# Two layer normalizations written by ScalarE with a scale and a bias from VectorE, in a gated cross-attention and mixture-of-experts kernel

## The chip, the cores and the metric

The kernel runs on one core of a Trainium2 chip. The metric is the device time of one execution in microseconds, as a median over runs. A second number, the span, is the time from the first to the last instruction in the trace of one profiled execution.

## What is computed

64 sequences of 128 tokens, 128 channels wide, go through a gated cross-attention and then a gated mixture of experts, each ahead of it a layer normalization. Cut to what matters:

```
def _layernorm(x, axis=-1, eps=1e-05):
    m = jnp.mean(x, axis=axis, keepdims=True)
    v = jnp.var(x, axis=axis, keepdims=True)
    return (x - m) / jnp.sqrt(v + eps)
...
x = x + jnp.tanh(g_xattn[0]) * _L0_xattn_ref(_layernorm(x, axis=-1), ctx_768, ...)   # 16 heads, 77 keys
x = x + jnp.tanh(g_ffn[0]) * _L0_ffn_ref(_layernorm(x, axis=-1), ...)
# _L0_ffn_ref: scores = softmax(flat @ router_w.T + router_bias); top 4 of 32 experts per token,
# their outputs weighted and summed, plus a shared expert
```

## The kernel before, in words

The program has two stages. In the first one (to about 571 us) a software pipeline goes over the 64 sequences, called batches here; the change touches this stage alone. The second stage reads the tokens back sorted by expert.

Each engine runs its own function `step(i, u, has)` for i from -2 to 66: the first six and the last seven steps are written out, the 56 between them are a hardware loop with four steps in its body. In one step the engines work on batches of different age: the normalization of batch i+2, keys and values of batch i+1, the scores of batch i, softmax and context of batch i-1, the second normalization of batch i-2, the routing of batch i-3. An engine takes its instructions in the order in which `step` writes them, and each waits for semaphores (`need(engine, semaphore, count)`). So the order in a step is fixed by hand, and an instruction that waits holds up all behind it on its engine.

The names that matter:

- First normalization: DVE gets mean and variance (`mv1`), ACT makes `rs1 = exp(-0.5 ln(var + eps))`, POOL subtracts (`xc`) and multiplies (`xn`). PE transposes `xn` one step later (L987).
- Second normalization: DVE makes `mv2`, ACT `rs2`, DVE writes four copies of the normalized rows into `payload[:, u]` (L753), one of two buffers. That write waits for `sent[u]`: the four scatters of the batch two before it, which read this buffer, must have landed.
- Routing of batch i-3: PE transposes `payload` (L976), ACT copies the result to `x2T`, PE multiplies with the router weights, DVE takes the top four, makes `onehot`, PE counts positions (L1012), DVE makes `pos`, POOL `prod`, DVE `slotf` and `slot`. POOL then scatters the four copies into `x_rows` by indirect DMA (L432).
- The order on PE in one step: scores (L968), transposition of `payload` (L976), keys and values (L958), the first of three groups of probability transpositions (L920), router (L982), transposition of `xn` (L987), the rest, and last the context matmuls (L943, L948).
- L987 writes the PSUM bank `ps_f` that also held keys and values, so it waits until DVE has copied these into `kvbd` (L679).
- On ACT the copy of the values into `vt` and `vtail` (L539, L543) waits for the last context matmul of the step (L948), as that reads the old ones.

Of the kernel before, what the change touches and what calls it, by code (L numbers as in the profile page):

```python
# [29 lines left out]
E, H = 32, 128  # L30
# [40 lines left out]
def build(nc, x, ctxT, wkv, wts, vecs, consts, gu, dn, out):  # L71
# [4 lines left out]
    with ExitStack() as stack:  # L76
        def sb(name, shape, dt=F32):
            return stack.enter_context(nc.sbuf_tensor(name, shape, dt))
# [4 lines left out]
        def sems(name, n=2):  # L83
# [28 lines left out]
        xc = sb("xc", [128, D])  # L112
# [23 lines left out]
        idxf = sb("idxf", [128, TOPK])  # L136
# [59 lines left out]
        names = ("st1_d mv1_d lv1_d rs1_d xc_d xn_d xnT_p xnT_d kv_p kv_d q_p q_d vt_p vt_d s_p mx_d mxc_d diff_d relu_d "  # L196
                 "pt_p pt_d pv_p rden_d on_d oT_p oT_d y_p xb_d x1_d st2_d mv2_d lv2_d rs2_d x2_d x2T_p x2T_d x2Ta_d "
                 "lg_p lg_d top_d ntop_d idx_d idxf_d oh_d pre_p pos_d base_d prod_d slotf_d slot_d e4_d "
                 "rse_d gate_d pidx_d dest_d")
        S = {n: sem(n) for n in names.split()}  # L200
        (st1_d, mv1_d, lv1_d, rs1_d, xc_d, xn_d, xnT_p, xnT_d, kv_p, kv_d, q_p, q_d, vt_p, vt_d, s_p, mx_d, mxc_d, diff_d,
         relu_d, pt_p, pt_d, pv_p, rden_d, on_d, oT_p, oT_d, y_p, xb_d, x1_d, st2_d, mv2_d, lv2_d, rs2_d,
         x2_d, x2T_p, x2T_d, x2Ta_d, lg_p, lg_d, top_d, ntop_d, idx_d, idxf_d, oh_d, pre_p, pos_d, base_d, prod_d,
# [181 lines left out]
        def _(pool):  # L385
# [9 lines left out]
            def step(i, u, has):  # L395
# [4 lines left out]
                if has(0):  # L400

                    need_first(pool, xn_d, i + 1)
                    xi = x_all[:, bass.ds(i * D, D)]
                    nc.gpsimd.tensor_tensor(xi, xi, bias2[:, :], ALU.add).then_inc(xb_d, 1)
                if has(2):
                    m = i + 2
                    need(pool, rs1_d, m + 1)
                    need(pool, xnT_p, m - 1)
                    need_first(pool, xn_d, m)
                    nc.gpsimd.tensor_tensor(xc[:, :], x_all[:, bass.ds(m * D, D)],  # L410
                                            mv1[:, u, 0:1].broadcast_to([128, D]), ALU.subtract).then_inc(xc_d, 1)
                    need(pool, xc_d, m + 1)
                    nc.gpsimd.tensor_tensor(xn[:, u, :], xc[:, :], rs1[:, u:u + 1].broadcast_to([128, D]),
                                            ALU.mult).then_inc(xn_d, 1)
                if has(-3):
                    m, v = i - 3, o

                    need(pool, pos_d, m + 1)
                    nc.gpsimd.tensor_tensor(prod[:, :, :], onehot[:, :, :],
                                            pos[:, :].unsqueeze(1).broadcast_to([128, TOPK, E]),  # L420
                                            ALU.mult).then_inc(prod_d, 1)
# [7 lines left out]
                                            ALU.add).then_inc(dest_d, 1)  # L429
                    need_first(pool, slot_d, m + 1)  # L430
# [29 lines left out]
        def _(act):  # L460
# [8 lines left out]
            def step(i, u, has):  # L469
# [64 lines left out]
                if has(0):  # L534
                    relu(1)
                if has(1):
# [9 lines left out]
                    r.then_inc(vt_d, 1)  # L546
                if has(-2):
# [64 lines left out]
        def _(dve):  # L612
# [25 lines left out]
            def step(i, u, has):  # L638
# [571 lines left out]
```

## Time and profile before

| | |
|---|---|
| device time, median of 3 runs | 1083.81 us (1083.36 to 1087.75) |
| the profiled execution: its own time | 1080.21 us |
| its span | 1078.3 us |
| mean granted TensorE clock | 0.976 |
| busy share of the span: PE, DVE, POOL, ACT | 88%, 68%, 63%, 57% |

The shares are averages over two stages with different limits; what the change is worth is read from the first stage alone. L12 is line 12 of the kernel's file, PE is TensorE's matmuls, PEld its weight loads, DVE VectorE, ACT ScalarE, POOL GpSimd. "x_rows<-payload,slot" reads: writes `x_rows`, reads `payload` and `slot`.

### The profile page before, as it was taken

The page shows a single profiled execution, that of the slowest core. Times are in us where ns is not written, and L with a number is a line of the kernel's source. Part 1 is how long each engine was busy: PE and PEld are TensorE (multiplying, and loading weights), DVE is VectorE, ACT ScalarE, POOL GpSimd, SP SyncE. Part 2 cuts the span into 40 slices and gives each one's busy share as a digit, 9 for nine tenths or more (in the row PEclk, how much of TensorE's full clock was granted, in tenths as well). Part 3 has the DMA queues.
Part 4 walks back from the last instruction along what each step waited for, and adds up shares of the span by engine and source line. Part 5 has one row for each costly group of instructions (what it writes and reads, how often), then busy time and mean ns, then how long its engine had stood idle before and what let it go on. Part 6 is the DMA issues. An engine that isn't in the chain of part 4 may idle for free.

```text
span 1078.3 us, 26023 instructions
## 1 busy us (share of the span) xinstructions
PE 954.1 (88%) x6592; PEld 727.2 (67%) x6593; DVE 736.7 (68%) x2513; ACT 613.7 (57%) x2213; POOL 682.5 (63%) x947
## 2 busy tenths in 40 slices
PE   4998888888888988888868999999999999999976
PEld 2777777777777777777654766666676676766544
DVE  3788898898888988988755444444444444444796
ACT  3676677777667777777531555555555555554111
POOL 1276777777767777777666476777777777777000
PEclk9999999999999999999869899999999999999999
DMA  5511111111111111112213333333333333330893
GB/s 157 194 40 33 34 39 38 33 39 38 33 33 37 40 33 36 38 35 73 100 37 99 97 99 93 93 93 90 95 93 94 92 93 93 91 96 23 299 363 118
DMA packets 90278, 90.42 MB, mean 84 GB/s; under 512 B 21277, under 2 KB 71562, under 8 KB 89860
## 3 DMA queue, kind: packets, MB, share of 16 engines
q1 hardware_dynamic: 72452, 55.34, 18.0%
q0 software_dynamic: 17792, 34.67, 9.9%
q8 instruction: 17, 0.28, 0.1%
q14 instruction: 17, 0.14, 0.0%
HBM read 49.72 MB, written 42.31 MB: 85 GB/s over the span
## 4 chain that ended last, share of the span: by engine, by line
PE 43%; issue 16%; DVE 16%; DMA 12%; POOL 10%; ACT 1%; POOLq 1%; SPq 0%; DVEq 0%; ACTq 0%
PE ps L1072 11%; DMA x_rows<-payload,slot 11%; POOL x_rows L432 9%; PE ps L1083 9%; DVE payload L753 3%; PE ps L1109 3%; PE ps L1067 3%; PE ps L1077 3%; PE ps L1099 3%; PE ps L1093 3%; PE ps L1036 2%; DVE kvbd L679 2%; PE ps L1045 2%; PE ps L943 1%; DVE x_all L886 1%
## 5 line engine op out<-in xcount | busy, mean ns | idle before, releaser
L450 POOL DMA_INDIRECT y_rows<-y_sb,xin x288 | 283.1, 983 | 127.6 <-issue 81.9
L432 POOL DMA_INDIRECT x_rows<-payload,slot x256 | 251.2, 981 | 130.2 <-DVE slot L764 67.9
L839 DVE TENSOR_TENSOR h<-sg,ps 128x128 f32<-128x128 f32 x288 | 82.8, 288 | 183.7 <-ACT sg L577 183.7
L1072 PE MATMUL ps<-w_gu,xT 128*128 x576 | 175.7, 387 | 8.3 <-issue 8.3
L1083 PEld LDWEIGHTS ps<-w_dn,hT 128*128 128x128 f32 x576 | 94.3, 189 | 106.0 <-ACT hT L582 73.5
L943 PE MATMUL ps<-vt,pT 128*128 128x108 f32 x1024 | 146.1, 288 | 0.0
L943 PEld LDWEIGHTS ps<-vt,pT 128*128 128x128 f32 x1024 | 131.0, 200 | 11.6 <-issue 11.2
L582 ACT COPY hT<-ps 128x128 f32<-128x128 f32 x288 | 76.4, 265 | 109.6 <-PE ps L1077 107.9
L1083 PE MATMUL ps<-w_dn,hT 128*128 x576 | 129.9, 307 | 8.0 <-DVE y_sb L845 6.0
L577 ACT ACTIVATE sg<-ps 128x128 f32<-128x128 f32 x288 | 80.5, 279 | 72.7 <-PE ps L1072 48.6
L845 DVE TENSOR_SCALAR y_sb<-ps,xin 128x128 f32<-128x128 f32 x288 | 100.0, 347 | 24.1 <-PE ps L1083 22.5
L476 ACT ACTIVATE prob<-prob 128x512 f32<-128x512 f32 x128 | 80.5, 630 | 61.7 <-DVE prob L713 60.2
L488 ACT ACTIVATE pT<-ps 128x512 f32<-128x512 f32 (+1 forms) x192 | 99.7, 519 | 7.7 <-PE ps L920 5.1
L668 DVE TENSOR_REDUCE mx<-ps 128x8 f32<-128x616 f32 x128 | 101.1, 789 | 4.2 <-PE ps L968 3.9
L713 DVE SCALAR_TENSOR_TENSOR prob<-ps,mxc 128x616 f32<-128x616 f32 x128 | 99.6, 779 | 0.1
L1072 PEld LDWEIGHTS ps<-w_gu,xT 128*128 128x128 f32 x576 | 87.8, 193 | 11.6 <-issue 11.6
L920 PE MATMUL ps<-cst,prob 128*128 128x128 f32 x512 | 81.4, 283 | 0.3 <-ACT pT L488 0.3
L1067 PE MATMUL ps<-cst,xin 128*128 128x128 f32 x288 | 79.2, 275 | 2.7 <-DMA xin<-x_rows 2.2
L572 ACT COPY xT<-ps 128x128 f32<-128x128 f32 x288 | 78.3, 272 | 5.4 <-PE ps L1067 5.4
L1077 PE MATMUL ps<-cst,h 128*128 128x128 f32 x288 | 78.8, 274 | 0.0
L987 PE MATMUL ps<-cst,xn 128*128 128x128 f32 x64 | 21.6, 337 | 59.3 <-DVE kvbd L679 59.3
L562 ACT ACTIVATE ssg<-ps 128x512 f32<-128x512 f32 x32 | 19.1, 597 | 81.2 <-PE ps L1036 81.2
(136 smaller groups left out, 2011.9 us busy)
## 6 DMA issues: line engine op xcount, KB each, us to landing
xin<-x_rows SPq DMA_DIRECT2D x288, 65.0 KB, 1.8
w_gu<-y_rows SPq DMA_DIRECT2D x16, 1024.0 KB, 7.7
y_rows<-y_sb,xin POOLq DMA_INDIRECT x288, 2.3
w_gu<-in_gu SPq DMA_DIRECT2D x2, 2048.0 KB, 9.6
x_rows<-payload,slot POOLq DMA_INDIRECT x256, 2.4
out<-x_all SPq DMA_DIRECT2D x16, 256.0 KB, 5.0
w_dn<-in_dn SPq DMA_DIRECT2D x1, 2048.0 KB, 8.5
ctx_sb<-in_ctxT SPq DMA_DIRECT2D x64, 29.2 KB
```

The lines of the kernel that those rows point to most:

```text
L432: nc.gpsimd.indirect_dma_start(x_rows, bass.IndirectOffsetOnAxis(ap=slot[:, v, k:k + 1], axis=0), payload[:, v, k, :], None).then_inc(sent ...
L450: nc.gpsimd.indirect_dma_start(y_rows, bass.IndirectOffsetOnAxis(ap=xin[:, u, D:D + 1].bitcast(U32), axis=0), y_sb[:, u, :], None, bounds_ ...
L488: nc.scalar.activation(pT[:, f, 0:n, :].rearrange("p a b -> p (a b)"), ps_p[:, 0:n * T], ACT.Exp, scale=-1.0).then_inc(pt_d, 1)
L668: nc.vector.reduce_max(mx[:, 2 * GH * n:2 * GH * (n + 1)].rearrange("p (g a) -> p g a", a=GH), ps[:, 2 * n:2 * n + 2, 0:GK].rearrange("p g ...
L713: nc.vector.scalar_tensor_tensor(out=prob[:, u, 2 * n:2 * n + 2, :].rearrange("p g (a k) -> p g a k", a=GH), in0=ps[:, 2 * n:2 * n + 2, 0: ...
L839: nc.vector.tensor_tensor(h[:, u % 2, :], sg[:, u % 2, :], ps_gu[u % 2][:, H:2 * H], ALU.mult).then_inc(h_d[u % PER], 1)
L845: nc.vector.tensor_scalar(y_sb[:, u % U3, :], ps_dn[:, 0:D], xin[:, u % U3, D + 1:ROW], None, ALU.mult).then_inc(y_d[u % PER], 1)
L943: r = nc.tensor.matmul(ps_o[:, at:at + 3 * GC], pT[:, f, n, :], vt[:, o, c, near:near + 3, :].rearrange("p g c -> p (g c)"), start=f == 0 ...
L1067: after(nc.tensor.transpose(ps_xT[:, 0:128], xin[:, u % U3, 0:D], ident), xin_in, n16, u).then_inc(xT_p[u % PER], 1)
L1072: after(nc.tensor.matmul(ps_gu[u % 2][:, 0:2 * H], xT[:, u % 2, :], w_gu[:, bass.ds(e * (2 * H), 2 * H)], start=True, stop=True), xT_d, n, ...
L1077: after(nc.tensor.transpose(ps_hT[:, 0:128], h[:, u % 2, :], ident), h_d, n, u).then_inc(hT_p[u % PER], 1)
L1083: after(nc.tensor.matmul(ps_dn[:, 0:D], hT[:, u % 2, :], w_dn[:, bass.ds(e * D, D)], start=True, stop=True), hT_d, n, u).then_inc(dn_p[u % ...
```

## The change

Both normalizations are applied by ACT in one instruction each, `Identity(scale * x + bias)`, with the per-row `rs` as scale and a per-row bias `nb = -mean * rs` that DVE makes in one small instruction. POOL loses `xc` and `xn`; DVE loses the write of `payload`, and with it the wait for `sent[u]`, which now stands ahead of ACT's write. On POOL the step of `dest` (the index field of the scattered row) stands ahead of `prod`. DVE compares with the unsigned top indices directly, without a cast to `idxf`. ACT's `relu_tails` of batch i runs at the end of step i instead of at the start of step i+1. PE's program is the same.

```
@@ gpsimd step @@
                 if has(0):
-                    need_first(pool, xn_d, i + 1)
+                    need(pool, xn_d, i + 1)
                     xi = x_all[:, bass.ds(i * D, D)]
                     nc.gpsimd.tensor_tensor(xi, xi, bias2[:, :], ALU.add).then_inc(xb_d, 1)
-                if has(2):
-                    m = i + 2
-                    need(pool, rs1_d, m + 1)
-                    need(pool, xnT_p, m - 1)
-                    need_first(pool, xn_d, m)
-                    nc.gpsimd.tensor_tensor(xc[:, :], x_all[:, bass.ds(m * D, D)],
-                                            mv1[:, u, 0:1].broadcast_to([128, D]), ALU.subtract).then_inc(xc_d, 1)
-                    need(pool, xc_d, m + 1)
-                    nc.gpsimd.tensor_tensor(xn[:, u, :], xc[:, :], rs1[:, u:u + 1].broadcast_to([128, D]),
-                                            ALU.mult).then_inc(xn_d, 1)
...
-                    need(pool, pos_d, m + 1)
-                    nc.gpsimd.tensor_tensor(prod[:, :, :], onehot[:, :, :], ...
...
                     nc.gpsimd.tensor_tensor(dest[:, v, :], dest[:, 1 - v, :], cst[:, C_STEP:C_STEP + TOPK],
                                             ALU.add).then_inc(dest_d, 1)
+                    need(pool, pos_d, m + 1)
+                    nc.gpsimd.tensor_tensor(prod[:, :, :], onehot[:, :, :], ...
@@ scalar step @@
+                if has(2):
+                    m = i + 2
+                    need(act, nb1_d, m + 1)
+                    need(act, xnT_p, m - 1)
+                    nc.scalar.activation(xn[:, u, :], x_all[:, bass.ds(m * D, D)], ACT.Identity, bias=nb1[:, u:u + 1],
+                                         scale=rs1[:, u:u + 1]).then_inc(xn_d, 1)
                 if has(1):
                     need(act, vt_p, i + 2)
                     need(act, pv_p, FILLS * i)
...
                     r.then_inc(vt_d, 1)
+                if has(-2):
+                    m = i - 2
+                    need(act, nb2_d, m + 1)
+                    need(act, sent[u], upto(m, u, 64))
+                    nc.scalar.activation(payload[:, u, :, 0:D],
+                                         x_all[:, bass.ds(m * D, D)].unsqueeze(1).broadcast_to([128, TOPK, D]),
+                                         ACT.Identity, bias=nb2[:, :], scale=rs2[:, :]).then_inc(x2_d, 1)
+                if has(0):
+                    relu_tails()
@@ vector step @@
-                if has(-3):
-                    need(dve, idx_d, i - 2)
-                    nc.vector.tensor_copy(idxf[:, :], idx[:, 0:TOPK]).then_inc(idxf_d, 1)
...
+                if has(2):
+                    m = i + 2
+                    need(dve, rs1_d, m + 1)
+                    need(dve, xn_d, m - 1)
+                    nc.vector.tensor_scalar(nb1[:, u:u + 1], mv1[:, u, 0:1], -1.0, rs1[:, u:u + 1], ALU.mult,
+                                            ALU.mult).then_inc(nb1_d, 1)
...
                     need(dve, rs2_d, m + 1)
-                    need(dve, sent[u], upto(m, u, 64))
-                    nc.vector.tensor_scalar(payload[:, u, :, 0:D], xi.unsqueeze(1).broadcast_to([128, TOPK, D]),
-                                            mv2[:, 0:1], rs2[:, :], ALU.subtract, ALU.mult).then_inc(x2_d, 1)
+                    need(dve, x2_d, m)
+                    nc.vector.tensor_scalar(nb2[:, :], mv2[:, 0:1], -1.0, rs2[:, :], ALU.mult,
+                                            ALU.mult).then_inc(nb2_d, 1)
```

On ACT, in the hardware loop, the end of a step before (`prob` is the second half of the softmax's relu, `vt` and `vtail` the copies of the values; REGISTER_ALU and ISA rows prepare counts and addresses; numbers at the end of names are left out, so `nb` is `nb1` or `nb2`):

```order
L476 ACTIVATE prob<-prob 128x2x256
L220 REGISTER_ALU
L539 COPY vt<-ps 128x8x32
L543 COPY vtail<-ps 52x2x32 x2
L551 COPY x2T<-ps 128x128
L552 ISA
L552 COPY x2T_all<-ps 128x128
```

And of the change, the same place:

```order
L466 ACTIVATE prob<-prob 128x2x256
L528 ISA
L528 ACTIVATE xn<-x_all,nb,rs 128x128
L220 REGISTER_ALU
L533 COPY vt<-ps 128x8x32
L537 COPY vtail<-ps 52x2x32 x2
L545 ISA
L545 ACTIVATE payload<-x_all,nb,rs 128x4x128
L471 ACTIVATE ptail<-prob 128x4x52
L554 COPY x2T<-ps 128x128
```

`xn` has come in ahead of the copies of the values, `payload` and the tails (`ptail`, before at the start of the next step) between these copies and `x2T`, which copies what PE makes of `payload`.

On DVE, in the hardware loop, the end of a step before:

```order
L713 SCALAR_TENSOR_TENSOR prob<-ps,mxc 128x616
L748 RECIPROCAL rse<-se 128x1
L220 REGISTER_ALU
L753 TENSOR_SCALAR payload<-x_all,mv,rs 128x4x128
L758 TENSOR_REDUCE slotf<-prod 128x4
L761 TENSOR_SCALAR payload<-e,rse,tg 128x4
L764 CAST slot<-slotf 128x4
```

And of the change:

```order
L713 SCALAR_TENSOR_TENSOR prob<-ps,mxc 128x616
L754 RECIPROCAL rse<-se 128x1
L759 TENSOR_SCALAR nb<-mv,rs 128x1
L764 TENSOR_REDUCE slotf<-prod 128x4
L767 TENSOR_SCALAR payload<-e,rse,tg 128x4
L770 CAST slot<-slotf 128x4
```

The write of 512 numbers a row has become one of a single number, and `slot` no longer stands behind a wait for scatters.

On POOL, in the hardware loop, a step before:

```order
L404 TENSOR_TENSOR x_all<-x_all,bias 128x128
L220 REGISTER_ALU
L410 ISA
L410 TENSOR_TENSOR xc<-x_all,mv 128x128
L413 TENSOR_TENSOR xn<-xc,rs 128x128
L419 TENSOR_TENSOR prod<-onehot,pos 128x128
L425 CAST payload<-dest 128x4
L428 TENSOR_TENSOR dest<-dest,cst 128x4
L432 DMA x_rows<-payload,slot 266368x130 x4
```

And of the change:

```order
L404 TENSOR_TENSOR x_all<-x_all,bias 128x128
L410 CAST payload<-dest 128x4
L413 TENSOR_TENSOR dest<-dest,cst 128x4
L416 TENSOR_TENSOR prod<-onehot,pos 128x128
L422 DMA x_rows<-payload,slot 266368x130 x4
```

Two instructions are gone, and `prod` is now the last one ahead of the scatters.

## Rows read from the trace of the kernel before

**Rows 1.** Busy us of PE, PEld, DVE, ACT, POOL; granted clock; DMA share; GB/s.

```profile
200.00:280.00 80.00, 71.11 (x640) 59.24 (x640) 70.83 (x269) 57.26 (x197) 59.83 (x100) 1.00 0.12 37
```

**Rows 2.** POOL in order of time: start us, us, line, [idle before <-releaser].

```profile
206.65 1.04 POOL L432 DMA_INDIRECT x_rows<-payload,slot  x1 [0.95 <-DVE slot L764]
...
211.50 0.47 POOL L404 TENSOR_TENSOR x_all<-x_all,bias 128x128 f32 x1
...
212.76 0.43 POOL L419 TENSOR_TENSOR prod<-onehot,pos 128x128 f32<-128x128 bf16 x1
213.13 0.39 POOL L425 CAST payload<-dest 128x4 uint32<-128x4 f32 x1
213.60 0.20 POOL L428 TENSOR_TENSOR dest<-dest,cst 128x4 f32<-128x4 f32 x1
214.75 1.04 POOL L432 DMA_INDIRECT x_rows<-payload,slot  x1 [0.95 <-DVE slot L764]
```

**Rows 3.** The chain that ended last, one link: start us, us.

```profile
210.53 2.29 DMA x_rows<-payload,slot
```

**Rows 4.** DVE in order of time, the same step and the next.

```profile
212.91 0.56 DVE L753 TENSOR_SCALAR payload<-x_all,mv,rs 128x512 f32 x1 [0.76 <-DMA x_rows<-payload,slot]
...
213.78 0.16 DVE L764 CAST slot<-slotf 128x4 uint32<-128x4 f32 x1
...
215.74 0.79 DVE L679 TENSOR_TENSOR kvbd<-ps,cst 128x616 f32<-128x616 f32 x1
...
218.04 0.27 DVE L699 CAST idxf<-idx 128x4 f32<-128x4 uint32 x1
...
220.05 0.77 DVE L713 SCALAR_TENSOR_TENSOR prob<-ps,mxc 128x616 f32<-128x616 f32 x1
```

**Rows 5.** PE in order of time, one step from its end to its end.

```profile
212.41 0.58 PE L948 MATMUL ps<-vtail,pT 128*128 128x72 f32 x4
...
213.65 0.33 PE L976 MATMUL ps<-cst,payload 128*128 128x128 f32 x1
213.87 0.64 PE L958 MATMUL ps<-ctx_sb,wkv_sb 97*128 97x77 f32 x4
...
216.58 0.33 PE L987 MATMUL ps<-cst,xn 128*128 128x128 f32 x1 [1.49 <-DVE kvbd L679]
...
221.02 0.58 PE L948 MATMUL ps<-vtail,pT 128*128 128x72 f32 x4
```

**Rows 6.** Groups by line, 100 to 440 us: busy us, mean ns | idle before.

```profile
L476 ACT ACTIVATE prob<-prob 128x512 f32<-128x512 f32 x82 | 51.7, 630 | 41.2 <-DVE prob L713 40.1
...
L753 DVE TENSOR_SCALAR payload<-x_all,mv,rs 128x512 f32 x41 | 24.0, 587 | 23.6 <-DMA x_rows<-payload,slot 23.1
...
L521 ACT ACTIVATE qT<-ps,bq_s 128x128 f32<-128x128 f32 x42 | 15.2, 361 | 0.0
...
L497 ACT ACTIVATE lv<-mv,eps 128x1 f32<-128x1 f32 x42 | 12.3, 294 | 2.3 <-DVE mv L663 2.3
...
L499 ACT ACTIVATE rs<-lv 128x1 f32<-128x1 f32 x42 | 8.5, 203 | 1.3
...
L693 DVE TENSOR_SCALAR ntop<-top 128x1 f32<-128x1 f32 x42 | 6.5, 154 | 1.4
```

**Rows 7.** ACT in order of time, the copies of the values and a relu.

```profile
213.03 0.37 ACT L539 COPY vt<-ps 128x256 f32<-128x256 f32 x1 [0.29 <-PE ps L948]
213.30 0.42 ACT L543 COPY vtail<-ps 52x64 f32<-52x64 f32 x2
...
220.85 0.63 ACT L476 ACTIVATE prob<-prob 128x512 f32<-128x512 f32 x1
```

**Rows 8.** ACT's copies of the values in step 2 and in step 59.

```profile
42.23 0.37 ACT L539 COPY vt<-ps 128x256 f32<-128x256 f32 x1 [0.49 <-PE ps L948]
...
508.09 0.37 ACT L539 COPY vt<-ps 128x256 f32<-128x256 f32 x1 [0.29 <-PE ps L948]
```

**Rows 9.** One of four stretches alike, columns as ahead.

```profile
84.60:88.00 3.40, 3.40 (x17) 3.27 (x17) 2.77 (x11) 1.67 (x6) 2.77 (x5) 0.50 0.18 58
```

More of the change, by code:

```diff
@@ L111, in build @@
         rs1 = sb("rs1", [128, 2])
-        xc = sb("xc", [128, D])
+        nb1 = sb("nb1", [128, 2])
+        nb2 = sb("nb2", [128, 1])
         xn = sb("xn", [128, 2, D])
@@ L135, in build @@
         idx = sb("idx", [128, 8], U32)
-        idxf = sb("idxf", [128, TOPK])
         onehot = sb("onehot", [128, TOPK, E], BF16)
@@ L195, in build @@
         ctx_in, sent = sems("ctx_in"), sems("sent")
-        names = ("st1_d mv1_d lv1_d rs1_d xc_d xn_d xnT_p xnT_d kv_p kv_d q_p q_d vt_p vt_d s_p mx_d mxc_d diff_d relu_d "
-                 "pt_p pt_d pv_p rden_d on_d oT_p oT_d y_p xb_d x1_d st2_d mv2_d lv2_d rs2_d x2_d x2T_p x2T_d x2Ta_d "
-                 "lg_p lg_d top_d ntop_d idx_d idxf_d oh_d pre_p pos_d base_d prod_d slotf_d slot_d e4_d "
+        names = ("st1_d mv1_d lv1_d rs1_d nb1_d xn_d xnT_p xnT_d kv_p kv_d q_p q_d vt_p vt_d s_p mx_d mxc_d diff_d relu_d "
+                 "pt_p pt_d pv_p rden_d on_d oT_p oT_d y_p xb_d x1_d st2_d mv2_d lv2_d rs2_d nb2_d x2_d x2T_p x2T_d x2Ta_d "
+                 "lg_p lg_d top_d ntop_d idx_d oh_d pre_p pos_d base_d prod_d slotf_d slot_d e4_d "
                  "rse_d gate_d pidx_d dest_d")
         S = {n: sem(n) for n in names.split()}
-        (st1_d, mv1_d, lv1_d, rs1_d, xc_d, xn_d, xnT_p, xnT_d, kv_p, kv_d, q_p, q_d, vt_p, vt_d, s_p, mx_d, mxc_d, diff_d,
-         relu_d, pt_p, pt_d, pv_p, rden_d, on_d, oT_p, oT_d, y_p, xb_d, x1_d, st2_d, mv2_d, lv2_d, rs2_d,
-         x2_d, x2T_p, x2T_d, x2Ta_d, lg_p, lg_d, top_d, ntop_d, idx_d, idxf_d, oh_d, pre_p, pos_d, base_d, prod_d,
+        (st1_d, mv1_d, lv1_d, rs1_d, nb1_d, xn_d, xnT_p, xnT_d, kv_p, kv_d, q_p, q_d, vt_p, vt_d, s_p, mx_d, mxc_d, diff_d,
+         relu_d, pt_p, pt_d, pv_p, rden_d, on_d, oT_p, oT_d, y_p, xb_d, x1_d, st2_d, mv2_d, lv2_d, rs2_d, nb2_d,
+         x2_d, x2T_p, x2T_d, x2Ta_d, lg_p, lg_d, top_d, ntop_d, idx_d, oh_d, pre_p, pos_d, base_d, prod_d,
          slotf_d, slot_d, e4_d, rse_d, gate_d, pidx_d, dest_d) = S.values()
@@ L429, in step @@
                                             ALU.add).then_inc(dest_d, 1)
+                    need(pool, pos_d, m + 1)
+                    nc.gpsimd.tensor_tensor(prod[:, :, :], onehot[:, :, :],
+                                            pos[:, :].unsqueeze(1).broadcast_to([128, TOPK, E]),
+                                            ALU.mult).then_inc(prod_d, 1)
                     need_first(pool, slot_d, m + 1)
@@ L478, in relu_tails @@
                 def relu_tails():
-                    need(act, diff_d, 2 * i)
+                    need(act, diff_d, 2 * i + 2)
                     need(act, pt_p, FILLS * (i - 1))
-                    nc.scalar.activation(ptail[:, o, :, 0:TAIL], prob[:, o, :, 128 * CH:GK], ACT.Relu,
+                    nc.scalar.activation(ptail[:, u, :, 0:TAIL], prob[:, u, :, 128 * CH:GK], ACT.Relu,
                                          scale=-1.0).then_inc(relu_d, 1)
@@ L705, in step @@
                     m = i - 3
-                    need(dve, idxf_d, m + 1)
+                    need(dve, idx_d, m + 1)
                     need(dve, pre_p, m)
                     nc.vector.tensor_tensor(onehot[:, :, :], iota.unsqueeze(1).broadcast_to([128, TOPK, E]),
-                                            idxf[:, :].unsqueeze(2).broadcast_to([128, TOPK, E]),
+                                            idx[:, 0:TOPK].unsqueeze(2).broadcast_to([128, TOPK, E]),
                                             ALU.is_equal).then_inc(oh_d, 1)
```

9 lines of the change are left out of this document (2 added, 7 removed).

## The prediction

> **What bounds the kernel now.** I read the stretches first: in the middle of the first stage PE is busy 71.1 us of 80, DVE 70.8, ACT 57.3, POOL 59.8 [rows 1]. No engine is full, two are near it, so the period of a step must come from a ring of waits. The chain that ended last names the ring, and the timeline gives its links. First scatter of a batch at 206.65 on POOL, of the next at 214.75 [rows 2]: a step takes 8.10 us. In between, the fourth scatter's transfer starts at 210.53 and takes 2.29 [rows 3], to 212.82; DVE, idle for 0.76 us, then writes `payload` from 212.91 to 213.47, and after `slotf` and the gate `slot` ends at 213.94 [rows 4]; 0.81 us later POOL starts the next first scatter. 3.88 + 2.29 + 0.09 + 0.56 + 0.47 + 0.81 = 8.10, closed. PE has slack in it: it waits 1.49 us ahead of L987 for `kvbd` [rows 5].
>
> **What the change takes out.** DVE's `payload` write, 0.59 us [rows 6], and its wait leave DVE; `slot` no longer stands behind the scatters' landing, so this ring opens. The cast to `idxf` (0.27 us in rows 4, on a step's DVE path) goes, `nb1` and `nb2` come, 0.15 us each like `ntop` [rows 6]; for DVE alone a gain of about 0.6 us a step with the wait not counted. POOL loses `xc` and `xn`, the whole stretch between the add's end at 211.97 and `prod` at 212.76 [rows 2]: 0.8 us. Work alone gives no new bound: ACT's 57.3 of 80 us is 5.8 us in a step of 8.10, and `xn` and `payload` (below) bring it to 7.1.
>
> **What it adds, and where that lands.** The two writes go to ACT. Relu over 512 numbers takes ACT 0.63 us there [rows 6, 7]. The new write also carries a bias and a scale from memory. A bias costs 0.09: Ln with one takes 294 ns, Exp without 203 on the same one-number rows [rows 6]. A scale from memory has no row; it lies between nothing and, as the nearest row, another 0.09, and I take that, being the same kind of operand. So `payload` 0.63 + 0.18 = 0.81 us (0.72 without a price for the scale, 0.63 with none for either), and `xn` as `qT`, which has a bias, 0.36 + 0.09 = 0.45 [rows 6].
>
> The Trainium skill ("ScalarE: Activation LUTs", What ACT_TABLE_LOAD costs) gives 93 ns for each operand read per partition, and 186 ns plus 0.833 ns an element for the rest. The bias rows agree, no row shows the scale; by that page `payload` would be an estimated 0.80 us and the sum below 0.01 less. Its Rules for kernel authors there say that add and multiply belong on VectorE, not ScalarE; the write at 0.59 on DVE against 0.81 points the same way, and the first rival shows when that would not matter.
>
> Price is not the point, place is. On ACT `payload` stands behind the copies of the values, and those wait for PE's last context matmul, L948: it ends at 212.99, `vt` starts at 213.03 [rows 5, 7]. PE's next instruction but the scores is L976, which reads `payload`; queued behind it are L958 (keys and values), the probability turns, the router and L987. DVE's `kvbd` waits for L958, L987 for `kvbd`. Before, DVE wrote `payload` apart from all that, and PE reached L976 at 213.65 after its scores with the tile ready. Now there is a ring through three engines, from L948 to the next L948:
>
> - L948 to `vt` 0.04; both `vtail` end at 213.72, 0.69 after `vt` starts [rows 5, 7];
> - `payload` on ACT 0.81;
> - to L976: between 0.05 (`kvbd` ends 216.53, L987 starts 216.58) and 0.18 (`payload` ended 213.47, L976 started 213.65, with PE's scores before it) [rows 4, 5]. The second is this very wait, so I take 0.15;
> - L976 to the end of L958, 213.65 to 214.51: 0.86;
> - to `kvbd` 0.05 as above, `kvbd` 0.79, to L987 0.05;
> - L987 to the end of L948, 216.58 to 221.60: 5.02, in which PE's own order sets the pace [rows 5].
>
> Sum 8.46 us. Every link is an engine's order or a semaphore the code has, so a step can't be shorter. It leaves `kvbd`, which before had DVE's order as its limit (L958 was over at 214.51, `kvbd` began at 215.74), waiting for PE, and hides what DVE gained: DVE now idles ahead of `kvbd`. The wait for the scatters isn't the last on ACT: they land at 212.82, 0.90 ahead of the end of `vtail` at 213.72, and earlier from now on. POOL's gain only lengthens its wait for `slot`.
>
> **The stage.** From step 2 to step 59 the copies of the values move from 42.23 to 508.09 us [rows 8]: 465.86 us for 57 steps, a mean of 8.17. That holds the start at under 8.10 (no scatter to wait for yet) and the slower steps where the granted clock was 0.50, the lower level of 1.2 GHz: four stretches of 3.4 us [rows 9], 13.6 us in which PE does half as much, 6.8 us late at most; as the new ring has PE in it, I count all of it. After: 57 x 8.46 + 6.8 = 489.0, 23.1 more. In the last seven steps and the second stage nothing else changes; behind the last attention `payload` is on the path with `nb2` ahead of it, 0.15 + 0.81 - 0.59, about 0.4 us in each of two steps, 1 us. Sum +24 us. The profiled execution's own 1080.2 us would become 1104.2; the median of the runs is 3.6 above it, so 1083.8 + 24 = 1108. The small prices are each at the upper one of their two ends, so I round to 1107.
>
> **Rivals.**
>
> 1. *The open ring pays, faster.* If `payload` were written by the time PE ends its scores, PE would lose nothing, and the next ring is POOL's: four scatters to the add, 206.65 to 211.50, 4.85; add 0.47; index and `dest` 0.47 + 0.20; `prod`, now last, 0.43; 0.05 to DVE; `slotf` to `slot` 0.47; 0.81 to the scatter [rows 2, 4]: 7.75, that is 0.35 less a step, 57 x 0.35 = 20, so about 1064 us. For it: POOL and DVE are relieved, and were in the ring. It decides where `payload` ends under 0.66 us after L948 (212.99 to 213.65); the copies of the values ahead of it alone take 0.73. Chance 0.05.
> 2. *Operands cost nothing.* `payload` 0.63, 0.05 to L976: a step of 8.18, 57 x 8.18 + 6.8 = 473.1, +7 and the 1: 1092. With one operand priced, 8.27 to 8.37, 1097 to 1103. Against: the Ln row. Chance 0.17 for 1090 to 1103.
> 3. *ACT is late by itself.* From `kvbd` (215.74) DVE runs to the end of the second `prob`, 220.82 [rows 4]: 5.08, less the cast's 0.27, plus `nb1`'s 0.15: 4.96. Relu 0.03 later, 0.63, then `xn` 0.45, then `vt`; two ends overlap by 0.1 as `vt` and `vtail` do [rows 7]. With the way back to `kvbd` (0.69 + 0.81 + 0.15 + 0.86 + 0.05): 8.43, and 8.63 without the overlap. At 8.63 the stage takes 498.7, +33 and the 1: 1118. Chance 0.08 above 1116.
> 4. *No change within 0.5%.* The wait for the scatters goes over to ACT and holds the same 8.10. That needs a landing 0.9 us later than now or a period that PE's slack of 1.49 swallows; the ring above has already spent that slack. Chance 0.06.
>
> The forecast itself, steps of 8.37 to 8.6, has 0.64.
>
> **How the numbers follow.** The range takes rival 2's bound at the low end, 1091, and rival 3's at the high end, 1116; outside lie rivals 1 and 4, the tail of 3 and a little of 2, about 2 in 10. What a measurement here can tell from no change is about 0.5%, 5.4 us. Slower by more: the forecast, rival 3 and nearly all of rival 2, 0.88. Within: rival 4 and the lowest end of 2, 0.07. Faster: 0.05.
>
> **What would show it.** In the changed trace: scatters of successive batches about 8.4 to 8.5 us apart; ACT's `payload` at 0.8 us, right behind `vtail`, with no wait for a DMA; PE idle ahead of L976 (PE there waits for ACT's `payload`, about 1.0 us: it comes 0.04 + 0.69 + 0.81 + 0.15 after L948, where the scores end 0.66 after it) and less than before ahead of L987; DVE idle ahead of `kvbd`, on PE, where it had no idle time; no wait of DVE for scatters; POOL waiting longer for `slot`. I am wrong if scatters come every 7.8 us, if PE never waits at L976, or if the chain still goes through the landing of `x_rows`.

## The result, and the profile after

The changed kernel takes 1134.4 us (1132.17 to 1135.3) against 1084.28 us, both medians of four runs: a ratio of 1.0451, with a 95% interval of 1.0428 to 1.0474. That is slower, as forecast, but by 50 us where 23 were forecast, and outside the range of 1091 to 1116.

The profiled execution took 1132.17 us, with a span of 1130.0 and a mean granted clock of 0.960 (before 0.976). Its page: busy time, the granted clock in 40 slices, and three groups (busy, mean ns | idle before, releaser):

```profile
PE 981.1 (87%) x6592; PEld 745.3 (66%) x6593; DVE 739.3 (65%) x2513; ACT 687.1 (61%) x2341; POOL 625.6 (55%) x819
...
PEclk9999899899998998999987999999999999999999
...
L422 POOL DMA_INDIRECT x_rows<-payload,slot x256 | 251.5, 982 | 179.9 <-DVE slot L770 116.2
...
L682 DVE TENSOR_TENSOR kvbd<-ps,cst 128x616 f32<-128x616 f32 x64 | 51.2, 799 | 67.7 <-PE ps L964 67.7
...
L982 PE MATMUL ps<-cst,payload 128*128 128x128 f32 x64 | 21.1, 330 | 70.6 <-ACT payload L545 70.6
```

The waits have changed places as forecast: PE waits for ACT's `payload` (70.6 us over 64 steps, 1.1 each), DVE's `kvbd` waits for PE (67.7), and between steps 2 and 59 nobody waits for scatters to land (ACT's `payload` does in two later steps, 2.69 and 0.83 us). What is new is the row of the clock: in the first stage four slices read 8, where before none did; the low ones at its end, 8 and 7, were there before as 8, 6 and 8.

The copies of the values in step 2 and in step 59 bound the first stage [rows 8]:

```profile
41.82 0.37 ACT L533 COPY vt<-ps 128x256 f32<-128x256 f32 x1
...
559.38 0.35 ACT L533 COPY vt<-ps 128x256 f32<-128x256 f32 x1
```

517.56 us for 57 steps against 465.86, 51.7 more. The span grew by 51.7 too (1130.0 against 1078.3). So the whole loss lies in these 57 steps, a mean of 9.08 us, and the task is to split it.

One step at full clock, link by link. PE in order of time, from the end of L954 (the last context matmul, L948 before) to the next (start us, us, line):

```profile
249.22 0.58 PE L954 MATMUL ps<-vtail,pT 128*128 128x72 f32 x4
...
251.66 0.33 PE L982 MATMUL ps<-cst,payload 128*128 128x128 f32 x1 [1.13 <-ACT payload L545]
251.82 0.57 PE L964 MATMUL ps<-ctx_sb,wkv_sb 97*128 97x77 f32 x4
...
253.29 0.33 PE L993 MATMUL ps<-cst,xn 128*128 128x128 f32 x1 [0.31 <-DVE kvbd L682]
...
257.89 0.58 PE L954 MATMUL ps<-vtail,pT 128*128 128x72 f32 x4
```

ACT in the same step:

```profile
250.09 0.35 ACT L533 COPY vt<-ps 128x256 f32<-128x256 f32 x1
250.34 0.42 ACT L537 COPY vtail<-ps 52x64 f32<-52x64 f32 x2
250.79 0.81 ACT L545 ACTIVATE payload<-x_all,nb,rs 128x512 f32 x1
...
257.85 0.63 ACT L466 ACTIVATE prob<-prob 128x512 f32<-128x512 f32 x1
258.38 0.48 ACT L528 ACTIVATE xn<-x_all,nb,rs 128x128 f32 x1
258.77 0.35 ACT L533 COPY vt<-ps 128x256 f32<-128x256 f32 x1
```

And DVE:

```profile
252.44 0.80 DVE L682 TENSOR_TENSOR kvbd<-ps,cst 128x616 f32<-128x616 f32 x1 [1.08 <-PE ps L964]
...
254.89 0.61 DVE L708 TENSOR_TENSOR onehot<-cst,idx 128x128 bf16<-128x128 f32 x1
...
257.05 0.77 DVE L713 SCALAR_TENSOR_TENSOR prob<-ps,mxc 128x616 f32<-128x616 f32 x1
```

The forecast ring is there: `payload` follows `vtail` on ACT, takes the 0.81 us that were forecast, PE's L982 starts 0.06 after it, L964 ends 0.73 later, `kvbd` starts 0.05 later. The first link is the one that reads otherwise. L954 ends at 249.80 and `vt` could start at 249.84; it starts at 250.09, 0.29 after that end, and no wait for PE stands beside it. ACT was busy with `xn`. The same a step later (258.47 and 258.77): `xn` stands behind the second relu, and this behind DVE's second `prob`, which ends at 257.82. So ahead of `vt` the path of the third rival ends last, from `kvbd` over DVE and ACT. On it one instruction is twice its length: `onehot` takes 0.61 us where it took 0.29.

The groups of DVE and of ACT between 100 and 530 us show the means (columns as in [rows 6]):

```profile
L703 DVE TENSOR_SCALAR mxc<-mx 128x16 f32<-128x16 f32 x48 | 20.3, 422 | 1.7
L708 DVE TENSOR_TENSOR onehot<-cst,idx 128x128 bf16<-128x128 f32 x48 | 17.5, 364 | 0.0
...
L730 DVE TENSOR_SCALAR nb<-mv,rs 128x1 f32<-128x1 f32 x48 | 9.6, 200 | 0.0
```
```profile
L545 ACT ACTIVATE payload<-x_all,nb,rs 128x512 f32 x47 | 38.3, 814 | 1.2
L528 ACT ACTIVATE xn<-x_all,nb,rs 128x128 f32 x47 | 22.5, 478 | 0.0
```

And the same two DVE groups of the kernel before, 100 to 460 us:

```profile
L708 DVE TENSOR_TENSOR onehot<-cst,idxf 128x128 bf16<-128x128 f32 x44 | 12.7, 289 | 0.0
...
L703 DVE TENSOR_SCALAR mxc<-mx 128x16 f32<-128x16 f32 x44 | 7.7, 175 | 0.0
```

`mxc` is the same instruction in both kernels and takes 0.42 us in place of 0.18; `onehot` 0.36 in place of 0.29. Together 0.32 us a step, on the path that ends last ahead of `vt`. POOL in another step and in the one above shows beside what:

```profile
217.47 0.96 POOL L422 DMA_INDIRECT x_rows<-payload,slot  x1 [0.30 <-issue]
218.45 0.46 POOL L404 TENSOR_TENSOR x_all<-x_all,bias 128x128 f32 x1
...
254.54 0.96 POOL L422 DMA_INDIRECT x_rows<-payload,slot  x1 [0.30 <-issue]
255.53 0.46 POOL L404 TENSOR_TENSOR x_all<-x_all,bias 128x128 f32 x1
```

`onehot` (254.89 for 0.61) ends at 255.50, and so does the fourth scatter of the batch on POOL (254.54 for 0.96); POOL's add starts 0.03 later. In the other step it is `mxc`:

```profile
217.94 0.49 DVE L703 TENSOR_SCALAR mxc<-mx 128x16 f32<-128x16 f32 x1
218.23 0.33 DVE L708 TENSOR_TENSOR onehot<-cst,idx 128x128 bf16<-128x128 f32 x1
```

It ends at 218.43, as the scatter does (217.47 for 0.96). Between 50 and 560 us `mxc` or `onehot` is lengthened by over 0.05 us and ends like this in 49 of 56 steps. In the kernel before, in this stage, one of 56 `mxc` and none of the `onehot` was; but 12 of the 56 casts to `idxf` were, up to 0.27 us from 0.16, and the one in [rows 4] is one of these.

PE is delayed by it too: its matmuls that count positions (L1018, L1012 before) load `onehot`. One row of the waits of PEld between 100 and 520 us (us in total, times, longest), where the kernel before has none for this line:

```profile
PEld ps L1018 <- issue: 5.6, 24, 0.3
```

"issue" doesn't name the releaser, but the times do. In the steps at full clock L1018 starts 0.40 to 0.41 us after `onehot` ends, whenever that end lies over 2.0 us behind the start of `xn`'s transposition on PE (L993), and the last context matmul ends 2.57 us after that start of L1018: with `onehot` ending 2.04 us behind L993 the stretch from L993 to the end of the step is 5.01, with 2.24 it is 5.21. With an earlier `onehot` the stretch stays at 5.02.

The second part is the clock. One of 18 stretches alike between steps 2 and 59 (columns as in [rows 1]; before there were four [rows 9]):

```profile
206.89:210.30 3.41, 3.41 (x18) 3.29 (x18) 3.05 (x11) 1.65 (x6) 2.34 (x5) 0.50 0.17 52
```

In the 26 steps that have no such stretch in them or in the step ahead, the period is a mean of 8.75 us. Its links, as means over these steps, beside the forecast's and those of three experiments below (worked out from the starts and ends of the same lines):

| link | forecast | after | `prod` first | `xn` behind | ring alone |
|---|---|---|---|---|---|
| last context matmul to `vt` | 0.04 | 0.27 | 0.17 | 0.04 | 0.04 |
| `vt` to `payload` | 0.69 | 0.70 | 0.70 | 0.72 | 0.72 |
| `payload` | 0.81 | 0.81 | 0.81 | 0.81 | 0.82 |
| to its transposition on PE | 0.15 | 0.07 | 0.07 | 0.07 | 0.09 |
| to the end of keys and values | 0.86 | 0.82 | 0.82 | 0.82 | 0.81 |
| to the end of `kvbd`, and to `xn`'s transposition | 0.89 | 0.89 | 0.89 | 0.89 | 0.89 |
| to the end of the last context matmul | 5.02 | 5.17 | 5.02 | 5.13 | 5.04 |
| sum | 8.46 | 8.73 | 8.48 | 8.48 | 8.41 |
| period measured | | 8.75 | 8.48 | 8.48 | 8.40 |

In the kernel after, five of the seven links stand within 0.01 us of the forecast or under it; the first and the last are longer. 57 x 8.75 = 498.8; the other 18.8 us of the 517.56 are the steps at the lower level of 1.2 GHz, about 1.0 us for each of the 18 stretches.

So three things stood to be told apart: the ring through ACT's `payload`, the lengthened DVE instructions beside POOL's scatter, and the clock.

### The profile page after: what moved, and what is told of

Its sections match the earlier page's. It is cut to its first block, busy times and chain, and to the rows that moved or that the text cites. A ratio compares the mean times of both kernels' runs of the same rounds, so it can differ in the third digit from the quotient of the medians.

```text
span 1130.0 us, 26020 instructions
## 1 busy us (share of the span) xinstructions
PE 981.1 (87%) x6592; PEld 745.3 (66%) x6593; DVE 739.3 (65%) x2513; ACT 687.1 (61%) x2341; POOL 625.6 (55%) x819
## 4 chain that ended last, share of the span: by engine, by line
PE 52%; DVE 20%; issue 13%; ACT 9%; POOL 3%; DMA 2%; ACTq 1%; DVEq 1%; SPq 0%; POOLq 0%
PE ps L1078 10%; PE ps L1089 9%; ACT payload L545 4%; PE ps L949 4%; DVE kvbd L682 4%; PE ps L964 3%; PE ps L1115 3%; DVE prob L713 3%; PE ps L1073 3%; PE ps L1083 2%; PE ps L1099 2%; PE ps L1105 2%; DVE mx L671 2%; PE ps L926 2%; DVE x_all L892 2%
## 5 line engine op out<-in xcount | busy, mean ns | idle before, releaser
L949 PE MATMUL ps<-vt,pT 128*128 128x108 f32 x1024 | 153.3, 298 | 0.0
L949 PEld LDWEIGHTS ps<-vt,pT 128*128 128x128 f32 x1024 | 139.0, 210 | 11.3 <-issue 11.3
L682 DVE TENSOR_TENSOR kvbd<-ps,cst 128x616 f32<-128x616 f32 x64 | 51.2, 799 | 67.7 <-PE ps L964 67.7
L926 PE MATMUL ps<-cst,prob 128*128 128x128 f32 x512 | 88.6, 301 | 0.3 <-ACT pT L478 0.3
L982 PE MATMUL ps<-cst,payload 128*128 128x128 f32 x64 | 21.1, 330 | 70.6 <-ACT payload L545 70.6
```

The lines of the kernel that those rows point to most:

```text
L926: r = nc.tensor.transpose(ps_p[:, n * T:(n + 1) * T], prob[:, o, g, 128 * c:128 * (c + 1)], ident)
L949: r = nc.tensor.matmul(ps_o[:, at:at + 3 * GC], pT[:, f, n, :], vt[:, o, c, near:near + 3, :].rearrange("p g c -> p (g c)"), start=f == 0 ...
```

## The experiments

All edits are to the kernel after, if nothing else is said. "Period" is the mean from copy to copy of the values in steps without a stretch of low clock in them or in the step ahead; "stage" the time from step 2 to step 59; both from the profiled execution. Ratios are to runs of the kernel before that were taken along with the experiment, with medians of 1080.97 us (first four experiments), 1083.89 (next four) and 1079.89 (last two).

**The normalized rows written by DVE again.** ACT's write goes, DVE's comes back with its wait for the scatters; the rest of the change stays.

```
-   nc.scalar.activation(payload[:, u, :, 0:D], ..., ACT.Identity, bias=nb2[:, :], scale=rs2[:, :])   # ACT
-   nc.vector.tensor_scalar(nb2[:, :], mv2[:, 0:1], -1.0, rs2[:, :], ALU.mult, ALU.mult)              # DVE
+   need(dve, sent[u], upto(m, u, 64))
+   nc.vector.tensor_scalar(payload[:, u, :, 0:D], ..., mv2[:, 0:1], rs2[:, :], ALU.subtract, ALU.mult)
```

> The changed kernel with one part undone: the write of payload is DVE's again, as before, with its wait for the scatters; xn on ACT, the order on POOL, the missing cast and the earlier tails stay. If the ring through ACT's payload is the cause, PE no longer waits for it at the transposition, the old ring through the scatters' landing closes again at about 8.10 us a step, the stretches at a granted clock of 0.50 fall from 18 in the first stage to about 4 to 6, and the time is 1078 to 1090 us. If the loss sits in the other parts (xn on ACT, the compare with unsigned indices, POOL's order), it stays above 1110.

Measured: 1079.44 us, 0.9979 (0.9959 to 0.9999) of before. The stage takes 465.86 us, as before, at a period of 8.10. DVE in order of time:

```profile
212.94 0.55 DVE L751 TENSOR_SCALAR payload<-x_all,mv,rs 128x512 f32 x1 [0.66 <-DMA x_rows<-payload,slot]
```

The wait of [rows 4] is back. The whole loss hangs on who writes `payload`: `xn` on ACT, the index field ahead of `prod` and the missing cast together cost nothing and bring nothing while this ring stands at 8.10.

**The cast of the top indices kept.** As before, DVE casts `idx` to `idxf` ahead of the comparison.

```
+   nc.vector.tensor_copy(idxf[:, :], idx[:, 0:TOPK])
-   nc.vector.tensor_tensor(onehot[:, :, :], ..., idx[:, 0:TOPK].unsqueeze(2)..., ALU.is_equal)
+   nc.vector.tensor_tensor(onehot[:, :, :], ..., idxf[:, :].unsqueeze(2)..., ALU.is_equal)
```

> The changed kernel with the cast of the top indices put back. In its trace mxc takes 0.42 us instead of 0.17 in the mean and onehot 0.36 instead of 0.29. If the compare with unsigned numbers is what is slow, both go back and the time falls to 1115 to 1122 us. If they are held up by POOL's fourth scatter (they end with it), the cast changes only who is held up: 1132 to 1142 us, with one of cast, mxc or onehot still ending together with the fourth scatter.

Measured: 1147.49 us, 1.0609 (1.0574 to 1.0645), above both. Its DVE groups between 100 and 540 us:

```profile
L712 DVE TENSOR_TENSOR onehot<-cst,idxf 128x128 bf16<-128x128 f32 x47 | 20.4, 434 | 0.6
L703 DVE CAST idxf<-idx 128x4 f32<-128x4 uint32 x47 | 19.0, 404 | 0.0
```

So `onehot` is not long because it compares unsigned numbers: with floats it takes 0.43 us here. The lengthening goes to whatever DVE runs at that moment, now to the cast too (0.40 against 0.18 in the kernel before). There are 26 stretches of low clock instead of 18. Dropping the cast was a help; without it the change would be worse.

**POOL's `prod` ahead of the add.** POOL's order becomes `prod`, add, index, `dest`, scatters; behind the fourth scatter now stands `prod`, which has to wait for DVE's `pos`.

```
+   need(pool, pos_d, m + 1)
+   nc.gpsimd.tensor_tensor(prod[:, :, :], onehot[:, :, :], ..., ALU.mult)
    need(pool, xn_d, i + 1)
    nc.gpsimd.tensor_tensor(xi, xi, bias2[:, :], ALU.add)
    ...
-   need(pool, pos_d, m + 1)
-   nc.gpsimd.tensor_tensor(prod[:, :, :], onehot[:, :, :], ..., ALU.mult)
```

> The changed kernel with POOL's step in the order prod, add, index, dest, scatters: what stands behind the fourth scatter is now prod, which waits for DVE's pos, and no longer the add, which is ready. If a ready POOL instruction behind the scatter is what holds up mxc and onehot on DVE, they take 0.17 and 0.29 again, the steps at full clock go from 8.67 to 8.81 down to 8.45 to 8.55, and the time is 1118 to 1127 us. If the unsigned compare or the scatter itself is the cause, nothing changes: 1130 to 1138.

Measured: 1107.96 us, 1.0246 (1.0211 to 1.0281): the right way, and further than expected. The period is the 8.48 expected; stretches of low clock fell from 18 to 7, which the expectation left as they were. POOL and then DVE in order of time:

```profile
216.69 0.96 POOL L424 DMA_INDIRECT x_rows<-payload,slot  x1 [0.30 <-issue]
220.15 0.43 POOL L403 TENSOR_TENSOR prod<-onehot,pos 128x128 f32<-128x128 bf16 x1 [2.50 <-DVE pos L746]
```
```profile
217.04 0.17 DVE L705 TENSOR_SCALAR mxc<-mx 128x16 f32<-128x16 f32 x1
217.13 0.29 DVE L710 TENSOR_TENSOR onehot<-cst,idx 128x128 bf16<-128x128 f32 x1
```

`mxc` and `onehot` now run inside the fourth scatter (216.69 to 217.65) at their old length, and `mxc` starts 0.35 us into it; in the row of the kernel after, where it was held, it starts 0.47 into it. A running scatter alone does not lengthen them there. In the table the last link is back at the forecast's 5.02, and the first has gone from 0.27 to 0.17; the rest of it, 0.13 over the forecast, the third rival's path has without any lengthening (forecast at 8.43 to 8.63 for the step).

**`xn` behind `payload` on ACT.** This takes `xn` off the way from the relu to `vt`.

```
-   nc.scalar.activation(xn[:, u, :], ...)     # between the second relu and vt
    ... vt, vtail, payload ...
+   nc.scalar.activation(xn[:, u, :], ...)
```

> The changed kernel with ACT's xn moved from ahead of the copies of the values to behind the write of payload. At full clock these copies start 0.29 us after the last context matmul instead of 0.04, behind xn. If that is part of the ring, they start 0.04 after it again, a step at full clock shortens by up to 0.25, and the time is 1118 to 1127 us. If the ring is closed elsewhere and xn only fills a wait, nothing changes: 1130 to 1138.

Measured: 1106.64 us, 1.0239 (1.0203 to 1.0275). Again lower than expected, with a period of 8.48 and 5 stretches. `vt` starts 0.04 us after the last context matmul again (median; 0.29 in the kernel after), although `mxc` and `onehot` are still lengthened, to 0.26 and 0.39 on average. ACT in order of time:

```profile
257.36 0.63 ACT L466 ACTIVATE prob<-prob 128x512 f32<-128x512 f32 x1
258.16 0.37 ACT L527 COPY vt<-ps 128x256 f32<-128x256 f32 x1 [0.17 <-PE ps L954]
...
258.88 0.81 ACT L539 ACTIVATE payload<-x_all,nb,rs 128x512 f32 x1
```

ACT waits for PE ahead of `vt`, as the forecast had it. This cures the first link whole, and leaves the last at 5.13: PE still gets `onehot` late. That both cures give 8.48 is a coincidence of two different remainders, 0.13 in the first link there and 0.11 in the last here.

**PE kept busy while it waits.** Eight transposes of a constant, into a PSUM bank that is free then, ahead of the wait for `payload`. Nothing reads what they write.

```
+   for n in range(8):
+       nc.tensor.transpose(ps_p[:, n % 4 * T:(n % 4 + 1) * T], ident, ident)
    need(pe, x2_d, i - 2)
```

> The changed kernel with eight extra transpositions of the identity on PE, into the bank that the probability transpositions overwrite next, ahead of the wait for payload (1.13 us at full clock; the eight take about 0.9). Nothing waits for them. If the 18 stretches at a granted clock of 0.50 come from PE standing still there, they fall to 6 or fewer, a step at full clock stays at 8.67 to 8.81 us, and the time falls to 1112 to 1123 us although PE does more. If they come from something else, they stay and the time is 1130 to 1140.

Measured: 1112.61 us, 1.0261 (1.0212 to 1.0309), some 22 us less than the kernel after with 512 transposes more. The period is a mean of 8.76 over all 57 steps, and no stretch of low clock is left: 499.12 us for the stage, against 517.56. PE in order of time, and the page's row of the clock:

```profile
252.05 1.09 PE L981 MATMUL ps<-cst 128*128 128x128 f32 x8
253.25 0.33 PE L984 MATMUL ps<-cst,payload 128*128 128x128 f32 x1
```
```profile
PEclk9999999999999999999998999999999999999999
```

The eight lie where PE stood idle for 1.13 us. The ring is not touched, so it is the clock alone that gives 18.4 us back in the stage.

**Only the write of `payload` on ACT.** The kernel before, with this one write moved behind ACT's copies of the values, with `nb2` and the wait for the scatters.

```
-   nc.vector.tensor_scalar(payload[:, u, :, 0:D], ...)                                  # DVE, before
+   nc.vector.tensor_scalar(nb2[:, :], mv2[:, 0:1], -1.0, rs2[:, :], ALU.mult, ALU.mult)
+   nc.scalar.activation(payload[:, u, :, 0:D], ..., bias=nb2[:, :], scale=rs2[:, :])    # ACT, behind vtail
```

> The kernel before with one part of the change: payload written by ACT behind the copies of the values, nb2 by DVE. xn stays on POOL, the cast, POOL's order and the place of the tails stay. If the ring through ACT's payload is the cause by itself, PE waits for ACT ahead of the transposition, a step at full clock is 8.4 to 8.6 us and the time 1100 to 1115. If it takes the other parts too, the time stays within 1075 to 1090.

Measured: 1140.91 us, 1.0528 (1.0488 to 1.0568): slower than expected, and slower than the whole change. `vt` follows the last context matmul by 0.04, but the period is 8.78, and 14 stretches are there. Its DVE groups between 100 and 530 us:

```profile
L711 DVE TENSOR_SCALAR mxc<-mx 128x16 f32<-128x16 f32 x47 | 27.7, 589 | 0.0
L716 DVE TENSOR_TENSOR onehot<-cst,idxf 128x128 bf16<-128x128 f32 x48 | 25.9, 539 | 0.4
```

They are the longest of all runs, 0.66 us over the kernel before; POOL still has `xc` and `xn` behind the add here, and 33 of 56 `mxc` and 23 of the casts last beyond the scatter, to the end of that add. They act through PE: the last link of the ring is 5.42 us here on average, up to 6.0 where `onehot` ends 3.0 us behind L995 (L993 in the kernel after), and all others are as in the kernel with `xn` behind. One row of the waits of PEld, 100 to 520 us (us in total, times, longest):

```profile
PEld ps L1020 <- DVE onehot L716: 13.5, 16, 1.0
```

L1020 are the matmuls that count positions; their loads wait for `onehot` up to 1.0 us. The rest of the change doesn't cause the loss, then; it takes a little of it away.

**Four buffers for the scattered rows, kernel before.** `payload`, `slot` and the semaphores `sent` fourfold, so that the write waits for the scatters of the batch four before it instead of two.

```
-   payload = sb("payload", [128, 2, ...   sems("sent")      slot = sb("slot", [128, 2, TOPK], U32)
+   payload = sb("payload", [128, 4, ...   sems("sent", 4)   slot = sb("slot", [128, 4, TOPK], U32)
```

> The kernel before with four buffers of payload and slot instead of two: DVE's write then waits for the scatters of the batch four before it, long landed. If the landing of the scatters closes the ring of before (8.10 us), its wait is gone and the next ring is POOL's, through prod and slot back to the scatters, at 7.87 us: 1066 to 1076 us. If another ring stands at 8.10 too, 1078 to 1084.

Measured: 1070.51 us, 0.9869 (0.9831 to 0.9906). The number is the expected one, the reason isn't: the stage still takes 466.13 us, at a period of 8.11. The gain is behind it: from the copy in step 59 to the last scatter 53.16 us pass instead of 62.90, and behind the last scatter both kernels take 507 us. POOL and then DVE in order of time show why the stage stays:

```profile
209.57 0.96 POOL L433 DMA_INDIRECT x_rows<-payload,slot  x1 [0.31 <-issue]
210.56 0.46 POOL L404 TENSOR_TENSOR x_all<-x_all,bias 128x128 f32 x1
...
211.92 0.42 POOL L419 TENSOR_TENSOR prod<-onehot,pos 128x128 f32<-128x128 bf16 x1
```
```profile
212.38 0.29 DVE L760 TENSOR_REDUCE slotf<-prod 128x4 f32<-128x128 f32 x1 [0.68 <-POOL prod L419]
```

POOL runs on without a wait to `prod`, DVE's `slotf` waits for it, and `slot` and the next scatter follow: a second ring, closed through POOL's own work. In this step it is 8.06 us from first scatter to first scatter (205.69 to 213.75), against 8.10 in [rows 2]: two rings within 0.05 us of each other. [rows 4] shows only the one that came last.

**Four buffers, and the rows written by DVE.** The same edit on the first experiment's kernel, where POOL has no `xc` and `xn`.

> The changed kernel with payload back on DVE, as in the run of that name, and four buffers of payload and slot. What POOL and DVE gained from the other parts can then shorten a step, as no wait for a landing is left: POOL's ring with prod last is 7.55 us with the index copy at its new 0.19 us, DVE's own work about 7.5. 1052 to 1068 us if so; 1074 to 1082 if the gains are lost to another ring.

Measured: 1054.0 us, 0.9730 (0.9691 to 0.9769): faster than both kernels, and the best version here. With both rings opened the period is 7.80, and one stretch of low clock is left. From `kvbd` to `kvbd` most steps take 7.57 to 7.84, but each fourth about 8.18. In one of the former DVE has next to no idle time, 0.19 us:

```profile
221.23 0.79 DVE L675 TENSOR_TENSOR kvbd<-ps,cst 128x616 f32<-128x616 f32 x1
...
222.30 0.19 DVE L687 MAX8 top<-lg 128x8 f32<-128x32 f32 x1 [0.19 <-DVE lg L681]
...
228.91 0.79 DVE L675 TENSOR_TENSOR kvbd<-ps,cst 128x616 f32<-128x616 f32 x1
```

228.91 - 221.23 = 7.68. DVE itself is the bound in such a step; what makes each fourth one longer is open.

**The add later on POOL.** Order index, `dest`, add, `prod`, scatters: behind the fourth scatter stands the index field (128x4) in place of the add (128x128), and it too is ready.

```
+   index, dest
    nc.gpsimd.tensor_tensor(xi, xi, bias2[:, :], ALU.add)
-   index, dest
    nc.gpsimd.tensor_tensor(prod[:, :, :], ...)
```

> The changed kernel with POOL's step in the order index, dest, add, prod, scatters: behind the fourth scatter now stands the copy of the index field, which is ready like the add was. If any POOL instruction that is ready and works on SBUF holds up DVE's mxc and onehot there, they still end with the fourth scatter, mxc stays near 0.42 us in the mean and the time is 1128 to 1140 us. If it was the add in particular, the time falls to that of the order with prod first, 1104 to 1110.

Measured: 1105.19 us, 1.0229 (1.0196 to 1.0262), period 8.49, 5 stretches. It is the second of the two expectations: not any ready instruction behind the scatter holds DVE up, the add does. `mxc` runs free in 39 of 52 steps, `onehot` in all. In the other 13 `mxc` ends with the scatter still. They differ by their place in it: they start 0.52 to 0.58 us after the scatter, the free ones up to 0.48 after it (two at 0.76 and 0.85). And the add matters at the same place: of the `mxc` that start 0.30 to 0.50 us into the scatter all 27 run free here, and all 28 are held in the kernel after.

**The ring alone.** `prod` first, `xn` behind `payload`, and the eight transposes, all three.

> The changed kernel with prod first on POOL, xn behind payload on ACT and the eight extra transpositions on PE: what is left of the loss should be the ring from L948 through ACT's payload to L948 by itself. By the forecast's links it is 8.46 us, 57 x 8.46 = 482.2 from step 2 to step 59, no step there at a granted clock of 0.50, and the time 1096 to 1104 us. If the ring hides a further wait, the stage takes over 488 and the time is above 1106; if the parts overlap so that the ring is shorter than its links, under 1092.

Measured: 1090.85 us, 1.0089 (1.0057 to 1.0121). The period is 8.40 (8.36 to 8.61) in all 57 steps, no stretch of low clock, `mxc` and `onehot` at 0.175 and 0.288. This is the prediction's ring without the other two: 478.57 us for the stage, 12.7 more than before, against 57 x 8.46 = 482.2. The 0.06 a step come from the links between `payload` and the end of keys and values (0.90 together, forecast 1.01), less 0.05 that others are over. The last seven steps are 1.8 us shorter (61.11 from the copy in step 59 to the last scatter, before 62.90), which makes the 11 us. The result lies under the expected 1096 to 1104, by these two amounts, and under the 1092 that was given for a ring shorter than its links.

## Why the prediction was off

**What held.** The direction, its cause and its place. The ring from the copies of the values over ACT's `payload` to PE and back exists, and giving the write back to DVE gives the time back (1079.44). Alone it is 8.40 us, forecast 8.46. PE waits 1.13 us ahead of `payload` (forecast about 1.0), `kvbd` waits for PE, POOL for `slot`, nobody for scatters.

**The operands.** `payload` takes 0.81 us, as summed: a scale from memory costs what a bias does, and the second rival falls. `xn` takes 0.48, forecast 0.45 (`qT`'s row and 0.09 for the scale). The Trainium skill ("ScalarE: Activation LUTs", What ACT_TABLE_LOAD costs) gives 93 ns for each such operand; by that `payload` is an estimated 0.80, and the measured 0.81 agrees.

**The step that failed: "The stage", 57 x 8.46 + 6.8 = 489.0.** Measured 517.56, 28.6 more. Both of its terms were too small.

1. *8.46 should have been 8.75*: 57 x 0.29 = 16.5 us. By the table: 0.23 more in the first link, 0.15 in the last, 0.1 less between. The first is the third rival's path, priced at 8.43 with DVE's instructions at their old lengths and given 0.08. From `kvbd` to the end of the second `prob` DVE took 5.38 in the step shown, forecast 4.96; of the 0.42, 0.32 is `onehot`, 0.05 `nb1` (0.20, forecast 0.15 from `ntop`). The last link I had taken as "PE's own order sets the pace"; that holds only while `onehot` is there in time. Behind both is what the sum missed: a step with another period puts other instructions side by side. `mxc` and `onehot` fell, before, into the third scatter or between; now into the end of the fourth, ahead of the add. With that gone and `xn` off the path, 8.40 is left (1090.85 us).
2. *6.8 us of low clock should have been 18.8*: 12.0 us more. I carried the four stretches of before over. But the forecast itself made a step 0.36 us longer with PE's program the same, and so it was forecasting a PE that stands still longer in each step. By PE's starts and ends in the steps that a period counts, it stood idle 0.95 us a step before and 1.46 after. After it there are 18 stretches. That they come of PE standing still is shown by the eight transposes: none left, period unchanged, 18.4 us back in the stage. How many a given wait brings is not: with `prod` first PE waits almost as long ahead of `payload`, 1.0 us a step, and stands idle 1.34 in all, and has 7.

16.5 + 12.0 = 28.5 of the 28.6. The two are not independent: each cure of a link also cut the stretches, from 18 to 7 and to 5.

**What I took from the ring before.** The text called the ring of landing scatters "closed" at 8.10, and had the change take 0.8 us of POOL's work out of the way. It wasn't alone: four buffers open it, and the period stays at 8.11, as POOL's own work closes a second one. That did no harm to the sum, as the new ring is longer than both. But the first rival's 7.75 needed both of them open and `payload` off ACT's path, and this came close: 7.80 with DVE writing.

PE's slack, 1.49 us by [rows 5], was that of one step, and among the longest. Its row of the waits before, 100 to 440 us (us in total, times, longest), gives a mean of 0.99:

```profile
PE ps L987 <- DVE kvbd L679: 41.5, 42, 1.5
```

**Left open.** By what means a scatter, and the add behind it, reach DVE, what makes each fourth step longer with four buffers and DVE writing, and how many stretches of low clock a wait of PE brings.

## What to carry to other kernels

An instruction is cheap or dear by what queues behind it on its engine and who waits there: 0.6 us of work moved from DVE to ACT cost 50 us, since on ACT it stood behind a copy that waits for the last matmul of a step. When a change alters the period of a software pipeline, sum the runner-up paths with what can newly fall beside them, and take a new wait on PE as a possible fall of the clock, priced from the stretches that the trace shows. And before a ring of waits is opened, look for the second one of nearly the same length: here two buffers' worth of waiting and POOL's work each had to go before a step got shorter, and then the kernel took 30 us less.

## What the runs showed of the hardware

**A DVE instruction held to the end of a scatter's issue.** `mxc` (0.18 us) and `onehot` (0.29) last until POOL's fourth `DMA_INDIRECT` ends, up to 0.32 us longer in the rows shown, when POOL's 128x128 add stands ready behind it. When the instruction starts decides. Over the first stage of all kernels here, with the add behind the scatter, the 82 `mxc` that start up to 0.29 us after it run free, and all 122 that start 0.30 to 0.73 after it are held. With `prod`, the index copy or another scatter behind it, the 305 that start within 0.50 us run free, and all 21 that start 0.51 to 0.71 after it are held too, to 0.01 to 0.03 us ahead of its end. The 12 lengthened casts of the kernel before are of this second kind. The Trainium skill ("SBUF — State Buffer", Who interferes with whom) has DVE and GpSimd share a pair of ports, locked for whole instructions, and names a copy, a cast or a `tensor_scalar` on DVE, where the operands meet its conditions, and one with two SBUF inputs, as those that can want it. `mxc`, the cast and `onehot` are of these kinds. But by that section whoever is first has the pair for its whole instruction, and here DVE was held before the add had started, or ran free inside a scatter; what passes between a scatter, the instruction behind it and DVE the runs don't show.

**Short waits of PE are enough to lower the clock.** Waits of 1.1 and 0.3 us in a step of 8.75 went with 18 stretches of 3.4 us at 1.2 GHz in 57 steps, where before, with one wait of 0.99 us on average in a step of 8.1, there were four. Needless transposes for 1.09 us in the place of the wait left none in the stage and made the kernel 22 us faster.
